# Second layer's attention: the next tile's first scores go ahead of a tile's last weighing, the last query is cut in halves, and the last projection waits for one addition less

## The reference

```python
q = (hidden_states @ Wq.T).reshape(b, s, H, D)          # 32 heads of 128
k = (k_cmp @ Wk_up.T).reshape(b, s, HK, D)              # 8 key/value heads
v = (v_cmp @ Wv_up.T).reshape(b, s, HK, D)
k, v = repeat(k, 4), repeat(v, 4)
scores = einsum('bhqd,bhkd->bhqk', q, k) * scale        # causal mask
attn = softmax(scores)
out = einsum('bhqk,bhkd->bhqd', attn, v)
return out.reshape(b, s, H * D) @ Wo.T
```

## Time and profile before

| what | value |
|---|---|
| three runs | 2376.98, 2381.04, 2386.32 us (median 2381.04) |
| the profiled execution's own time | 2381.8 us |
| its span, first to last instruction | 2380.0 us |
| mean granted clock of TensorE | 0.979 |
| PE busy | 2239.7 us, 94% |
| DVE, ACT, POOL busy | 65%, 45%, 43% |
| one iteration of batch 1 | 113.2 us |

### The profile page before, as it was taken

The page is one execution under the profiler, slowest core; times in us unless marked ns, Lnnn a source line. Parts: engine busy times, 40 slices in busy tenths (PEclk is TensorE's granted clock), DMA queues, the critical chain, the costliest instruction groups (busy, mean ns, idle before and its releaser), DMA issues. The chain is left out here.

```text
span 2380.0 us, 34649 instructions
## 1 busy us (share of the span) xinstructions
PE 2239.7 (94%) x11190; PEld 1815.5 (76%) x11190; DVE 1543.0 (65%) x3824; ACT 1069.2 (45%) x2275; POOL 1012.8 (43%) x1124
## 2 busy tenths in 40 slices
PE   6898898999999999999997987999999999999998
PEld 5554676888888888877785765888888888888886
DVE  6777565777777777756565464656565666666665
ACT  2456333545554454535353331545454545454444
POOL 5430714444445363767663010625353434434341
PEclk9899999999999999999998998999999999999999
DMA  9500573010101111020201282010101010101000
GB/s 347 203 1 10 211 269 117 10 62 9 62 19 52 32 39 45 26 68 20 70 6 54 118 319 79 18 54 26 62 9 62 9 62 9 62 9 62 27 32 32
DMA packets 74168, 165.26 MB, mean 69 GB/s; under 512 B 4721, under 2 KB 38897, under 8 KB 67442
## 3 DMA queue, kind: packets, MB, share of 16 engines
q1 hardware_dynamic: 73650, 162.95, 19.5%
q10 hardware_dynamic: 432, 1.32, 0.1%
HBM read 113.40 MB, written 72.61 MB: 78 GB/s over the span
## 5 line engine op out<-in xcount | busy, mean ns | idle before, releaser
L1776 DVE TENSOR_TENSOR pT<-psum,pT 128x512 fp32r<-128x512 f32 x576 | 386.8, 688 | 258.1 <-ACT pT L1824 255.8
L1676 POOL TENSOR_TENSOR probs_even<-probs_even,rinv 128x1024 f32<-128x1024 f32 (+2 forms) x192 | 241.1, 1257 | 572.3 <-DVE rinv L1767 572.2
L1824 ACT ACTIVATE pT<-psum 128x512 fp32r<-128x512 f32 x576 | 329.2, 596 | 307.8 <-PE psum L1885 307.7
L1762 DVE CUSTOM_DVE_ANT_0 psum<-psum,causal 128x256 f32<-128x256 f32 (+7 forms) x512 | 385.6, 767 | 35.6 <-PE psum L97 31.8
L1815 ACT ACTIVATE probs_even<-psum,nmax 128x1024 f32<-128x1024 f32 (+3 forms) x256 | 204.5, 799 | 247.0 <-DVE nmax L1762 243.6
L1676 POOL TENSOR_TENSOR probs_odd<-probs_odd,rinv 128x896 f32<-128x896 f32 (+2 forms) x192 | 198.6, 1042 | 246.9 <-DVE rinv L1767 246.9
L95 PE MATMUL psum<-keys,q 128*128 128x512 f32 (+3 forms) x768 | 265.5, 346 | 3.7 <-DVE q L1717 2.8
L97 PE MATMUL psum<-keys,q 128*128 128x512 f32 (+3 forms) x768 | 262.1, 341 | 0.0
L96 PE MATMUL psum<-keys,q 128*128 128x512 f32 (+3 forms) x768 | 261.8, 341 | 0.0
L95 PE MATMUL psum<-pT,vals 128*128 128x512 f32 x576 | 256.3, 445 | 4.2 <-DVE pT L1776 0.4
L1815 ACT ACTIVATE probs_odd<-psum,nmax 128x896 f32<-128x896 f32 (+3 forms) x256 | 176.7, 691 | 148.1 <-DVE nmax L1762 145.2
(11 more groups left out here) (299 smaller groups left out, 4441.0 us busy)
## 6 DMA issues: line engine op xcount, KB each, us to landing
k_parts<-kv_out SPq DMA_DIRECT2D x32, 512.0 KB, 4.5
wq<-wq_copy SPq DMA_DIRECT2D x16, 1024.0 KB, 4.8
wo<-wo_copy SPq DMA_DIRECT2D x16, 1024.0 KB, 4.8
v_parts<-kv_out SPq DMA_DIRECT2D x32, 512.0 KB, 4.0
keys<-k_parts SPq DMA_DIRECT2D x32, 512.0 KB, 4.5
vals<-v_parts SPq DMA_DIRECT2D x64, 256.0 KB, 3.0
acc<-in_x SPq DMA_DIRECT2D x4, 1024.0 KB, 12.1
xn_later<-xn SPq DMA_DIRECT2D x1, 2048.0 KB, 14.3
```

The lines of the kernel that those rows point to most:

```text
L1676: pool.tensor_tensor(p, p, rinv[:, u, h:h + 1].to_broadcast([P, (TB - u) * P]), ALU.mult).then_inc(p_ok, 1)
L1762: dve.tensor_tensor_reduce(out=row, in0=row, in1=causal[:, S - n:S], scale=-1.0, scalar=-2 * MASKED, op0=ALU.add, op1=ALU.min, accum_out=n ...
L1776: dve.tensor_tensor(pT[:, n % PT_SLOTS, 1, :], bank[T_BANK + n % 2], f32(pT[:, n % PT_SLOTS, 0, :]), ALU.subtract).then_inc(t_lo, 1)
L1824: act.activation(pT[:, n % PT_SLOTS, 0, :], bank[T_BANK + n % 2], ACT.Copy).then_inc(t_hi, 1)
```

## The change

In `steps`, `scores(u, 0)` of rounds 2 to 7 no longer opens the round: it is emitted in the round before, ahead of the last step of `rest`, which is the tile's last `weigh`. That holds for rounds 1 to 6, which emit the scores of tiles 2 to 7. In the last stage of an iteration the query that was cut into chunk 0 and chunks 1 to 3 (3 and 9 matmuls) is cut into two and two (6 and 6). And the projection of tile 7 waits for the addition of tile 5 rather than of tile 6.

```diff
@@ -1523,7 +1523,8 @@
                 for k in range(n):
                     rest += turns[k + LAG:k + LAG + 1] + [("weigh", u - 1, k)]
                 first, second = len(rest) // 3, len(rest) * 2 // 3
-                scores(u, 0, 1)
+                if u == 1:
+                    scores(u, 0, 1)
                 scores(u, 1)
                 if u == 1:
                     order.append(("wo parts", 0))
@@ -1548,7 +1549,9 @@
                         order.append(("wo parts", 2))
                     if u == 3 and not last:
                         order.append(("wq parts", 3))
-                    run(rest[second:])
+                    run(rest[second:-1])
+                    scores(u + 1, 0, 1)
+                    run(rest[-1:])
                     if u == 1:
                         order.append(("wo parts", 3))
                 else:
@@ -1900,7 +1903,7 @@
                         if u == 0:
                             pe.wait_ge(wo_ok, it * REP + REP)
                         pe.wait_ge(o_lo, it * TB + (O0 + u + 1))
-                        pe.wait_ge(x_add, it * TB + (X0 + u))
+                        pe.wait_ge(x_add, it * TB + (X0 + min(u, TB - 2)))
                         if u == 0 or 3 <= u < TB - 2 and not last:
                             pe.wait_ge(q_lo, it * QS + (2 * REP + max(u - 2, 0)))
                         mm3(pe, w_bank(u), [(oT[:, u % 2, 0, h * P:(h + 1) * P], oT[:, u % 2, 1, h * P:(h + 1) * P],
@@ -1917,9 +1920,9 @@
                         if u < QS - 1:
                             queries(u, range(CH)).then_inc(q_mm, 1)
                         elif u == QS - 1:
-                            queries(u, range(1))
+                            queries(u, range(CH // 2))
                         else:
-                            queries(int(u), range(1, CH)).then_inc(q_mm, 1)
+                            queries(int(u), range(CH // 2, CH)).then_inc(q_mm, 1)
```

## The result

The changed kernel takes 2441.52 us (median of 4 runs, 2440.16 to 2445.93) against 2381.07 us: a ratio of 1.0251, with a 95% interval of 1.0238 to 1.0264. It is slower by 60 us; 68 were forecast, and the time lies in the range of 2422 to 2467. Its profiled span is 2438.7 us against 2380.0. A full iteration of batch 1 takes 117.3 us instead of 113.2.

What follows compares the result with a forecast made beforehand. PE was taken as the bound. A full iteration, 3.44 + 1.67 - 0.35 = 4.76 us longer, gave 12 x 4.76 + 2 x 2.62 + 2 x 2.8 = 68 us, so 2449 us, range 2422 to 2467.

Steps and rivals of the forecast that it cites:

- What bounds: One iteration of batch 1: PE is busy 112.1 of 113.1 us, so only its waits can be won or lost.
- The removed waits: Last weighing of tiles 0 to 2: the moved score covers PE's waits, 3 x 0.35 = 1.05 us shorter per iteration.
- The chain through ACT: Projections of tiles 0 to 2 wait for scaling, maximum, exp, then heads' copy: 1.30, 1.07, 1.07 us later, together 3.44.
- Rounds 4 to 6: Projections of tiles 3 to 5, behind queries, come 0.26, 0.44 and 0.97 us later, together 1.67 us per iteration.
- The last stage: End of an iteration: the wait before tile 6's projection goes and the last projection skips the addition; 0.35 us won.
- Iterations 5 and 6 of batch 0: PE's 2.7 us wait for POOL at tile 3 absorbs the delays of tiles 1 and 2, leaving 2.62 us each.
- The last iterations: The two iterations without queries: tiles 0 to 2 cost 3.44 us, the end wins 0.60; 2.8 us longer each.
- that only the removed waits would count: ACT or DVE reach the moved work early enough, no new wait; 20 us won, so 2361 us; chance 4%.
- the rival with half of the loss: The projection waits, but other PE waits shrink or DVE's queue has drained; 28 us slower, so 2409; chance 8%.
- The rival of the clock: TensorE's clock falls in one of three new waits in each of 14 iterations; 24 us more, 2473; chance 10%.

Runs made afterwards that it cites:

- the run that moves only the exp: Changed kernel, but on ACT the exp of the moved head 0 stands behind the copy of the heads; 2379.8 us, ratio 0.9992 to the kernel before.
- the kernel with rounds 1 to 3 and the exp behind: Changed kernel, but head 0 moved in rounds 1 to 3 only, its exp behind the copy of the heads; 2356.6 us, ratio 0.9903 to the kernel before.

## Why the prediction was right

- **What bounds.** Right: PE is the bound and only its waits moved; its busy time in an iteration rose by 0.6 us, the idle time by 3.6.
- **The removed waits.** Right: the starts in the weighings of tiles 0 to 2 are 0.23 us apart, and 3 x 0.35 us are won. With the exp out of the way and the rounds with queries left alone, the iteration went from 112.67 (end's edits alone) to 111.63 us, 1.04.
- **The chain through ACT.** Right in mechanism, and shown by the run that moves only the exp. Its size was 3.44 us forecast against 2.94. At tile 1 the chain from the start of the scaling (1664.93) to the projection (1668.54) took 3.61 us where the sum had 3.89. The scaling took 0.62 and not 0.69. The maximum started 0.08 before the end shown for the scaling (1665.47), where the sum had it 0.03 behind; at tile 0 it is the same, 0.07 before (1648.35 + 1.10 against 1649.38). From the maximum to the exp and from the exp to the copy it took 0.92 and 0.78 for 0.91 and 0.80, and from the copy to the projection 1.37 for 1.46 (1.50 at tile 0). So the size that was most off is the hand-over on DVE, 0.10 to 0.11 in each chain.
- **Rounds 4 to 6.** Right: 1.67 us forecast, 1.66 measured, and 1.7 between the runs with and without them.
- **The last stage.** Right in sign, 0.35 against 0.49. Not foreseen for the sum was that the query in halves is worth nothing unless the wait for the addition goes, though the numbers for it were there; the run of the halves showed it.
- **Iterations 5 and 6 of batch 0.** Forecast 2.62 us each. From heads to heads they took 1.8 us more (120.0 and 120.1 against 118.2 and 118.3). That the wait for POOL takes up a part is right in sign, but the rows behind it were read for one of the two only. In iteration 6 the kernel before waits 2.5 and then 1.7 us for POOL, with the clock at 1.00 behind both; the changed kernel waits 1.9 us once, and the clock falls.
- **The last iterations.** Forecast 2.8 us each. In batch 1, from the copy of tile 0's heads to the end, it took 83.7 us against 81.6, 2.1 more. In batch 0, from that copy to the first one of batch 1, it took only 0.55 more (290.08 against 289.53). The clock lies in both numbers, and the sum had no term for it: in batch 0 it fell twice in this iteration of the kernel before (0.61 from 1279.8 to 1284.2, and 0.61 in the last projection) and not once in the changed one, in batch 1 not at all before and once in the changed one (0.72 from 2408 to 2414, behind a wait of 2.0 us).
- **The total.** It came out nearer than its terms, and that part is luck. For the 68 us of the sum its terms measured 49.3 (12 x 4.11), 3.6 and 2.6, which is 55.5 of the 58.7 us between the spans. The other 3 us had no term: the full iterations of batch 0 lost up to 0.8 us more each than those of batch 1, 1.8 in all, and 1.3 lie ahead of the first heads, which is within what that start varies.
- **The rivals.** That only the removed waits would count is what the kernel with rounds 1 to 3 and the exp behind showed, so the rival described what the edit could give, not what it gave. Of the rival with half of the loss little is seen: the wait before the sixth turn stayed (0.3 us in the list), and 4.11 us of an iteration were lost, not 2. The rival of the clock is refuted for the full iterations: it stayed at 1.00 through waits of 1.2 to 1.6 us in each (2.38 us from transposes to projection at tile 0 for the usual 0.79, 1.95 at tile 1 and 2.06 at tile 2). But the reason given against it was weaker than it looks. It rested on the last iteration of batch 1, and at the same place in batch 0, behind waits of up to 1.2 us too, the kernel before has this stretch (columns as in the earlier trace rows):

```profile
1279.80:1284.20 4.40, 4.40 (x16) 0.61 0.00 0
```

So that these waits would leave the clock alone did not follow from the rows. In iteration 6 of batch 0 it did fall where it had not before, behind the wait of 1.9 us for POOL (changed kernel, same columns):

```profile
1156.00:1160.00 4.00, 4.00 (x13) 3.16 (x12) 1.39 (x4) 1.59 (x4) 1.31 (x2) 0.57 0.28 82
```

## What to carry to other kernels

When a step is moved ahead on the engine that is the bound, list what it issues on the other engines, and look for a short operation there that the bound engine needs soon and that now stands behind a long one it needs late. An engine that is idle half of the time can still be the cause, if it waits at the head of its queue. Here a move that fills three waits of 0.35 us opened three of 1.2 to 1.6; with one exp set behind a copy the same move won.

## What the runs showed of the hardware that was not expected

A wait of PE can cost more than its own length. The first matmul behind one starts the next 0.31 to 0.33 us later, where 0.23 is usual (1618.30 in the earlier trace rows to the row below, kernel before), and taking away a wait of 0.22 us gave 0.33.

```profile
1618.63 0.39 PE L96 MATMUL psum<-pT,vals 128*128 128x512 f32 x1
```

It is not the wait alone that does this. The first matmul behind transposes shows the same where there is no wait, so at tile 6's projection, which stands behind transposes, nothing of it is won: 0.33 with the wait (1692.45 to 1692.78, before) and 0.32 without (1726.86 to 1727.18, changed).

The length of a wait alone did not decide the granted clock behind it. At the last projection of a batch, which each of the eleven profiles of this study has twice, a wait of 1.57 us (from the starts) was followed by 1.00 all 16 times. One of 2.26 us was followed by 0.61 to 0.62 in batch 0 of the kernel before and of the query in halves, and by 1.00 in batch 0 of the moved scores alone and in batch 1 of all three. In the last iteration of batch 0 the clock fell behind one of 1.2 us in the kernel before and stayed at 1.00 behind one of 2.4 us in the changed one. At the first turn of tile 3 in iterations 5 and 6 of batch 0 a wait of 1.9 us was followed by a fall in the changed kernel, both times, and by 1.00 with the moved scores alone, both times. What decides it was not isolated.
